# Graph layer with a feed-forward block: one one-hot for each gathered chunk, a VectorE lead of 20 products, a message ring of 16

## The chip, the cores and the metric

The kernel runs on one core of one Trainium2 chip. The metric is device time in microseconds (us), as the median of several executions. The profile shows one execution. Its engines are PE (TensorE, matmuls; PEld is its weight load), DVE (VectorE), ACT (ScalarE), POOL (GpSimd) and SP (SyncE).

## What is computed

12,500 nodes with 256 features each, and 212,500 edges (200,000 and one self loop for each node), sorted by destination. Cut to what matters:

```
xn  = layernorm(x)
agg = segment_sum(edge_weight[:, None] * xn[src], dst)     # the gather and scatter
gnn = relu(((1 + eps) * xn + agg) @ W1.T + b1) @ W2.T + b2
mix = hyperbolic mixer of xn (1x1 convolutions, batch norm over nodes, tanh/atanh maps)
x   = x + gnn + mix
x   = x + ffn(layernorm(x))   # top half of the nodes by a routing weight: gelu(. @ w1 + b1) @ w2 + b2
```

## The kernel before, in words

The nodes are worked through in 49 steps of 256 nodes (two tiles of 128 rows). The edges of a step lie in a window of 35 chunks of 128 edges. The 256 destinations of a step fall into four quarters of 64. For each chunk, POOL gathers 128 rows of `xn` from HBM into a buffer of the ring `msg` (an indirect DMA, L936). DVE makes a one-hot, 128 edges by 64 destinations, times the edge weights, in the ring `sel` (`edge` in `main_vector`, L1131). PE multiplies one-hot (as weights, 128x64) by messages (128x256) and sums into the quarter's 64 partitions of the bank `agg` (`edge` in `main_tensor`, L1328). One such pair of quarter and chunk is a **product**; the table `PRODUCTS` has 45 for a step. A quarter of an even number is side 0 (output partitions 0 to 63), one of an odd number side 1 (64 to 127). Chunks 7 to 9, 15 to 18 and 24 to 26 reach two quarters, so that 35 chunks make 45 products.

- The order of PE is written out by hand: `step` in `main_tensor` sends products up to certain counts (`PE_AT`) and puts the other work between: `mix_qkv` (L1351, L1352) at 0 and 12, `tail_supT` (L1380) at 0, `tail_w1` (L1388) at 2, `tail_w2` (L1397) at 6, `mix_h1` (L1342) at 16, 22 and 25, `mix_outT` (L1362) at 18 and 28, `mix_ft` (L1372) at 20 and 32, and the feed-forward block (L1423, L1435) at 28, 32, 35, 38, 41 and 45. I call what lies between two such counts a **burst**: products 0 and 1, 2 to 5, 6 to 11, and so on, the last one 41 to 44.
- 42 steps hold a feed-forward block (`FFN_AT`); steps 0, 1, 8, 17, 26, 35 and 44 don't, and their products 32 to 44 are one burst. Seven blocks stand behind the last step.
- The order of DVE is a loop over k = 0 to 44: at k it first makes the one-hot of product k + `LEAD` (12), then the work that `DVE_AT` puts at k: `take_sup` (L1188, the sums of the step before with the node's own row) at 0, `add_b2` (L1193) at 4, `mix_f` (L1178 to L1182) at 5, `ffn_result` (L1111) at 6, `mix_scale` (L453 to L455, L1138) at 6 and 12, `combine` (L1198 to L1203) at 7 and 15, `mix_recip`, `mix_ratio`, `mix_om` (L1143 to L1155) at 8 to 10 and 16 to 18, `mix_c` (L453, L1162, L1163) at 15 and 22, `mix_ft` (L1167) at 17 and 36, `tail_out` (L1214 to L1217) at 25 and 30, and the conversion of the next window's destinations (L1122) at 30.
- POOL gathers in the order in which the products first name the chunks (`GATHERS`); a chunk's number in it is its **place** (0 to 34). Gather number G may overwrite a buffer when the chunk that is `RING` (18) gathers back, and all before it, are done with (`FREED`, counted by the semaphore `slot_used`). The one-hot ring has `SEL_RING` (22) buffers of 64 columns.

The line that sets how far DVE may run ahead of PE, and the one that sets POOL's:

```
dve.wait_ge(slot_used, RING + max(0, at_ - SEL_RING + 1))
pool.wait_ge(slot_used, RING + back * STEP_PRODUCTS + FREED[m] + 1)
```

Of the kernel before, what the change touches and what calls it, by code (L numbers as in the profile page):

```python
# [7 lines left out]
ALU = mybir.AluOpType  # L8
ACT = mybir.ActivationFunctionType
F32 = mybir.dt.float32  # L10
# [4 lines left out]
P = 128  # L15
D = 256
# [3 lines left out]
HC = HID // P  # L20
RING = 18
SEL_RING = 22
LEAD = 12
EARLY_EDGES = 12
WINDOWS = 2
# [15 lines left out]
def products():  # L41


    order = []
    for h in range(2):
        for left, right in itertools.zip_longest(LEFT[h], RIGHT[h]):
            order += [(2 * h + side, k) for side, k in enumerate((left, right)) if k is not None]
    return order


PRODUCTS = products()
STEP_PRODUCTS = len(PRODUCTS)
GATHERS = list(dict.fromkeys(k for _, k in PRODUCTS))
PLACE = {k: n for n, k in enumerate(GATHERS)}
LAST_USE = {k: max(n for n, (_, kk) in enumerate(PRODUCTS) if kk == k) for k in GATHERS}
FIRST_OF = {q: min(n for n, (qq, _) in enumerate(PRODUCTS) if qq == q) for q in range(4)}
LAST_OF = {q: max(n for n, (qq, _) in enumerate(PRODUCTS) if qq == q) for q in range(4)}
FREED = [max(LAST_USE[k] for k in GATHERS[:n + 1]) for n in range(SLOTS)]


# [15 lines left out]
def build(nc, a, out):  # L76
# [3 lines left out]
    NS = NT // 2  # L80
# [8 lines left out]
    with ExitStack() as ctx:  # L89
        def sb(name, shape, dt=F32):  # L90
            return ctx.enter_context(nc.sbuf_tensor(name, shape, dt))
# [20 lines left out]
        window_dst = [sb(f"window_dst{b}", [P, SLOTS]) for b in range(WINDOWS)]  # L112
        rings = sb("rings", [P, RING * D + SEL_RING * P // 2])
        msg = [rings[:, D * q:D * (q + 1)] for q in range(RING)]
        H = P // 2
        sel = [rings[:, RING * D + H * q:RING * D + H * (q + 1)] for q in range(SEL_RING)]
        rem_msg = sb("rem_msg", [P, D])
# [674 lines left out]
        def x3_rows(m, h):  # L792
# [3 lines left out]
        DVE_AT = dict(scale=(6, 12), out=(8, 16), c=(15, 22), ft=(17, 36), sup=0, n4=1, f=5, y=6, x=4,  # L796
                      combine=(7, 15), rstd=20, tail_out=(25, 30), stage=30)

# [315 lines left out]
        def main_vector(dve):  # L1114
# [10 lines left out]
            def edge(i, n):  # L1125
                b, at_ = i % WINDOWS, i * STEP_PRODUCTS + n
                q, k = PRODUCTS[n]
                dve.wait_ge(slot_used, RING + max(0, at_ - SEL_RING + 1))
                if n == 0:
                    dve.wait_ge(dst_ready, i + 1)  # L1130
                v.tensor_scalar(sel[at_ % SEL_RING], iota[:, q * H:(q + 1) * H], window_dst[b][:, k:k + 1],  # L1131
                                window[b][:, k, 2:3].bitcast(F32), ALU.is_equal, ALU.mult).then_inc(sel_ready, 1)

# [86 lines left out]
            def step(i, j, mm):  # L1220
                mix = Link(dve, mix_link, MIX_LINKS, i)
                tail = Link(dve, tail_link, TAIL_LINKS, j)
                last = i == NS - 1
                for k in range(STEP_PRODUCTS):
                    if k == DVE_AT["stage"] and not last:
                        start_step(i + 1)
                    ahead = k + LEAD
                    nxt = ahead >= STEP_PRODUCTS
                    if not (last and nxt) and not (i == 0 and ahead < EARLY_EDGES):
                        edge(i + nxt, ahead % STEP_PRODUCTS)  # L1230
# [64 lines left out]
        def main_tensor(pe):  # L1295
# [20 lines left out]
            def edge(i, n):  # L1316
# [6 lines left out]
                if n == STEP_PRODUCTS - 1:  # L1323
                    remainder(i, 0)
                    remainder(i, 1)
                pe.wait_ge(sel_ready, i * STEP_PRODUCTS + n + 1)
                pe.wait_ge(msg_landed[gathered % RING], 16 * (gathered // RING + 1))
                te.matmul(agg[h][side * H:(side + 1) * H], sel[(i * STEP_PRODUCTS + n) % SEL_RING], msg[gathered % RING],  # L1328
                          start=first, stop=n == STEP_PRODUCTS - 1, skip_group_check=True).then_inc(slot_used, 1)
# [474 lines left out]
```

## Time and profile before

| | |
|---|---|
| median of 3 runs | 2653.31 us (2650.08 to 2653.38) |
| the profiled execution | 2652.74 us, its span 2651.0 us |
| PE busy | 2470.1 us (93%) |
| DVE busy | 1848.6 us (70%) |
| POOL busy | 1668.7 us (63%) |
| ACT busy | 1433.9 us (54%) |
| mean granted clock of PE | 0.982 |

The span runs from the first to the last instruction; 1.7 us of the execution lie around it. "Busy" is the union of an engine's instructions. A row of the waits tells how long an engine sat idle and what ended it; a row of the chain of waits is a piece of the path that ended last.

### The profile page before, as it was taken

What the parts mean: (1) busy time and instruction counts of PE and PEld (TensorE: products, weight loads), DVE (VectorE), ACT (ScalarE), POOL (GpSimd) and SP (SyncE); (2) the same over time, 40 slices, a digit from 0 to 9 for tenths busy, and PEclk for the clock granted to TensorE, in tenths of its full rate; (3) what the DMA queues carried; (4) which work ended last, traced back from release to release, by engine and by line L of the source; (5) the groups of instructions that cost most, each with busy time, mean ns of one, the idle gap of its engine ahead of it and who ended that gap; (6) DMA issues with size and microseconds to landing.
All of it is one profiled execution on the core that took longest, in us unless ns stands there. A gap on an engine that the chain in (4) does not pass through costs nothing.

```text
span 2651.0 us, 44955 instructions
## 1 busy us (share of the span) xinstructions
PE 2470.1 (93%) x13536; PEld 1775.5 (67%) x13536; DVE 1848.6 (70%) x6385; ACT 1433.9 (54%) x3219; POOL 1668.7 (63%) x1834
## 2 busy tenths in 40 slices
PE   4778999999999998999999999999899999999997
PEld 4665667666666665666666666666666666666686
DVE  7857676776766768667667676676776766767657
ACT  3545564655645646556455565564555655656531
POOL 1246777767677677676676766767767667677500
PEclk9889999999999999999999999999999999999998
DMA  6733434434344344443343433434434334343338
GB/s 204 249 105 104 127 111 121 112 111 128 107 113 117 103 123 115 114 118 107 111 120 108 131 110 109 119 105 116 121 112 118 111 107 120 109 131 110 93 115 276
DMA packets 225221, 327.46 MB, mean 124 GB/s; under 512 B 80846, under 2 KB 168511, under 8 KB 224957
## 3 DMA queue, kind: packets, MB, share of 16 engines
q0 software_dynamic: 84656, 231.94, 30.7%
q1 hardware_dynamic: 140300, 92.36, 11.6%
q8 instruction: 122, 2.00, 0.3%
q14 instruction: 143, 1.16, 0.1%
HBM read 285.70 MB, written 38.45 MB: 122 GB/s over the span
## 4 chain that ended last, share of the span: by engine, by line
PE 70%; DVE 20%; ACT 4%; DMA 3%; issue 2%; SPq 0%; DVEq 0%
PE bank L1328 16%; PE qkv L1423 13%; PE bank L1435 12%; PE bank L1342 8%; PE bank L1372 7%; DVE rings L1131 4%; PE qkv L1352 3%; DMA work<-in_x 3%; PE bank L1388 2%; PE bank L1397 2%; PE qkv L1351 2%; PE bank L1362 1%; DVE work L525 1%; DVE work L496 1%; DVE work L1198 1%
## 5 line engine op out<-in xcount | busy, mean ns | idle before, releaser
L936 POOL DMA_INDIRECT rings<-xn_dram,window x1715 | 1641.1, 957 | 753.6 <-issue 384.7
L1328 PE MATMUL bank<-rings 128*64 128x256 f32 x4410 | 700.8, 395 | 23.8 <-DVE rings L1131 21.9
L1131 DVE TENSOR_SCALAR rings<-iota,window_dst,window 128x64 f32<-128x64 f32 x2205 | 610.5, 332 | 32.5 <-PE bank L1328 17.8
L1328 PEld LDWEIGHTS bank<-rings 128*64 128x64 f32 x4410 | 302.9, 136 | 313.0 <-issue 121.3
L1435 PE MATMUL bank<-ffn_weights,work 128*128 128x256 f32 x1568 | 375.1, 388 | 0.0
L1423 PE MATMUL qkv<-work,ffn_weights 128*128 128x256 f32 x1568 | 367.3, 382 | 0.0
L1435 PEld LDWEIGHTS bank<-ffn_weights,work 128*128 128x128 f32 x1568 | 286.8, 190 | 82.0 <-issue 32.3
L1423 PEld LDWEIGHTS qkv<-work,ffn_weights 128*128 128x128 f32 x1568 | 290.4, 190 | 51.8 <-ACT work L1026 16.1
L1026 ACT ACTIVATE work<-qkv,fb 128x256 f32<-128x256 f32 x392 | 159.7, 472 | 303.2 <-PE qkv L1423 302.6
L1342 PE MATMUL bank<-resident,weights 128*128 128x256 f32 x1176 | 295.3, 394 | 0.0
L1342 PEld LDWEIGHTS bank<-resident,weights 128*128 128x128 f32 x1176 | 213.2, 191 | 79.2 <-issue 55.7
L1008 ACT ACTIVATE work<-bank 128x512 f32<-128x512 f32 x49 | 29.3, 597 | 433.6 <-PE bank L1380 394.7
L1351 PE MATMUL qkv<-ident,work 128*128 128x128 f32 x588 | 166.5, 283 | 62.5 <-ACT work L972 61.4
L1188 DVE SCALAR_TENSOR_TENSOR work<-work,cols,bank 128x512 f32<-128x512 f32 x49 | 36.6, 748 | 257.3 <-PE bank L1328 257.3
L1352 PE MATMUL qkv<-weights,work 128*128 128x128 f32 x1176 | 209.5, 282 | 0.0
L953 ACT ACTIVATE work<-qkv 128x1536 bf16<-128x1536 f32 x98 | 142.2, 1451 | 122.7 <-PE qkv L1352 122.7
L1372 PE MATMUL bank<-weights,work 128*128 128x256 f32 x784 | 195.7, 393 | 11.1 <-DVE work L1198 8.7
L1039 ACT ACTIVATE work<-bank,cols 128x256 f32<-128x256 f32 x294 | 149.8, 565 | 76.7 <-PE bank L1342 76.7
L1352 PEld LDWEIGHTS qkv<-weights,work 128*128 128x128 f32 x1176 | 186.8, 200 | 3.1
L1372 PEld LDWEIGHTS bank<-weights,work 128*128 128x128 f32 x784 | 141.6, 190 | 66.6 <-ACT work L983 34.9
L1351 PEld LDWEIGHTS qkv<-ident,work 128*128 128x128 f32 x588 | 86.5, 147 | 87.6 <-issue 85.0
L1193 DVE TENSOR_TENSOR work<-work,b_row 128x512 f32<-128x512 f32 x49 | 34.2, 698 | 135.0 <-DMA work<-in_x 134.9
(261 smaller groups left out, 3296.8 us busy)
## 6 DMA issues: line engine op xcount, KB each, us to landing
rings<-xn_dram,window POOLq DMA_INDIRECT x1715
xn_dram<-work SPq DMA_DIRECT2D x14, 896.0 KB, 8.7
work<-xn_dram SPq DMA_DIRECT2D x49, 256.0 KB
work<-in_x SPq DMA_DIRECT2D x48, 256.0 KB
out<-work SPq DMA_DIRECT2D x48, 256.0 KB
work<-in_x SPq DMA_DIRECT2D x7, 896.0 KB, 6.0
rings<-in_x SPq DMA_DIRECT2D x6, 896.0 KB, 10.9
rings<-out SPq DMA_DIRECT2D x6, 896.0 KB, 9.2
```

The costliest lines, as they stand in the source:

```text
L936: nc.gpsimd.indirect_dma_start(out=msg[G_ % RING][:, :], out_offset=None, in_=xn_dram[:, :], in_offset=bass.IndirectOffsetOnAxis(ap=window ...
L953: s.activation(sq_dump, qkv.rearrange("p r i s c -> p (r i s c)"), ACT.Square, accum_out=nsq[h]).then_inc(nsq_ready, 1)
L1026: ins = s.activation(hT[:, k], HID_BANK[q][:, e * D:(e + 1) * D], ACT.Gelu_apprx_tanh, bias=fb1[:, k:k + 1])
L1039: ins = s.activation(h2T[:, k], H1_BANK[q][:, e * D:(e + 1) * D], ACT.Relu, scale=bn_a[:, k:k + 1], bias=bn_b[:, k:k + 1])
L1131: v.tensor_scalar(sel[at_ % SEL_RING], iota[:, q * H:(q + 1) * H], window_dst[b][:, k:k + 1], window[b][:, k, 2:3].bitcast(F32), ALU.is_eq ...
L1328: te.matmul(agg[h][side * H:(side + 1) * H], sel[(i * STEP_PRODUCTS + n) % SEL_RING], msg[gathered % RING], start=first, stop=n == STEP_PR ...
L1342: ins = te.matmul(H1_BANK[q][:, e * D:(e + 1) * D], wqkvT[:, c, k * P:(k + 1) * P], h0T[:, c, 2 * i * P:2 * (i + 1) * P], start=(c == 0), ...
L1351: te.transpose(qkv[:, k // 2, k % 2, 0, :], lhs, ident[:, :])
L1352: ins = te.matmul(qkv[:, k // 2, k % 2, 1, :], lhs, mixW[:, k, :], start=True, stop=True)
L1372: ins = te.matmul(FT_BANK[h][:, 0:D], outT[:, c], wresT[:, c], start=(c == 0), stop=(c == 3))
L1423: ins = te.matmul(HID_BANK[q][:, e * D:(e + 1) * D], fw1[:, c, k * P:(k + 1) * P], x3T[:, c], start=(c == 0), stop=(c == C - 1))
L1435: ins = te.matmul(Y_BANK[:, h * D:(h + 1) * D], hT[:, k, h * P:(h + 1) * P], fw2[:, k], start=(k == 0 and h == 0), stop=(k == HC - 1), ski ...
```

## The change

- Each pair of products takes its side-1 product first (`products`). The order of the gathers changes with it.
- One one-hot for each chunk: where a chunk reaches two quarters, DVE makes it once, 128 columns wide, at the first of its two products, and nothing at the second. PE takes 64 of the columns for each product.
- The one-hot ring is 30 units of 64 columns, given out in a run by `one_hot_places`; a wide one takes two neighbouring units. A one-hot is held until its chunk's last product.
- `LEAD` is 20 in place of 12; one-hots for products 12 to 19 of step 0 are made ahead of the loop.
- The message ring has 16 buffers in place of 18 (the two rings together keep their size).
- The conversion of the next window's destinations moves from k = 30 to k = 22.

```
-RING = 18
-SEL_RING = 22
-LEAD = 12
+RING = 16
+SEL_UNITS = 30
+LEAD = 20
...
-            order += [(2 * h + side, k) for side, k in enumerate((left, right)) if k is not None]
+            order += [(2 * h + side, k) for side, k in ((1, right), (0, left)) if k is not None]
...
+FIRST_USE = {k: min(n for n, (_, kk) in enumerate(PRODUCTS) if kk == k) for k in GATHERS}
+REACHES = {k: sorted(q for q, kk in PRODUCTS if kk == k) for k in GATHERS}
...
+def one_hot_places(steps):
+    place, freed, holds, at = {}, {}, [-1] * SEL_UNITS, 0
+    for i in range(steps):
+        for k in GATHERS:
+            n = len(REACHES[k])
+            units = range(at % SEL_UNITS, at % SEL_UNITS + n)
+            assert units.stop <= SEL_UNITS
+            place[i, k], freed[i, k] = units.start, max(holds[u] for u in units) + 1
+            for u in units:
+                holds[u] = i * STEP_PRODUCTS + LAST_USE[k]
+            at += n
+    return place, freed
...
-                      combine=(7, 15), rstd=20, tail_out=(25, 30), stage=30)
+                      combine=(7, 15), rstd=20, tail_out=(25, 30), stage=22)
...
-                q, k = PRODUCTS[n]
-                dve.wait_ge(slot_used, RING + max(0, at_ - SEL_RING + 1))
+                if FIRST_USE[k] < n:
+                    return
+                quarters = REACHES[k]
+                dve.wait_ge(slot_used, RING + SEL_FREED[i, k])
...
-                pe.wait_ge(sel_ready, i * STEP_PRODUCTS + n + 1)
+                pe.wait_ge(sel_ready, gathered + 1)
```

The sequences that the table now gives for the end of a step, as (quarter, chunk), products 36 to 44:

```
before  (2,22) (3,34) (2,23) (3,24) (2,24) (3,25) (2,25) (3,26) (2,26)
change  (3,34) (2,22) (3,24) (2,23) (3,25) (2,24) (3,26) (2,25) (2,26)
```

PE, the last burst of a step with a feed-forward block (step 5), before; the number in `msg_landed` is the message buffer, so that 10 is chunk 25 and 11 is chunk 26:

```order
L1435 MATMUL bank<-ffn_weights,work 128x256 x3
L1328 MATMUL bank<-rings 64x256 [waits msg_landed10,sel_ready] x2
L1328 MATMUL bank<-rings 64x256 [waits msg_landed11,sel_ready]
L1311 TENSOR_LOAD work
```

The same place in the change; 14 is chunk 24, 0 is chunk 25 and 1 is chunk 26:

```order
L1463 MATMUL bank<-ffn_weights,work 128x256 x3
L1356 MATMUL bank<-rings 64x256 [waits msg_landed14,sel_ready]
L1356 MATMUL bank<-rings 64x256 [waits msg_landed1,sel_ready]
L1356 MATMUL bank<-rings 64x256 [waits msg_landed0,sel_ready]
L1339 TENSOR_LOAD work
```

Behind the register instructions that follow comes product 44, (2,26), in both. The burst was side 1, 0, 1, 0, with chunk 25 for both sides first; it is now side 0, 1, 0, 0.

DVE from the second `tail_out` (k = 30) to `take_sup` of the next step (k = 0), before:

```order
L1217 TENSOR_SCALAR route_w<-work,cols 128x1
L1131 TENSOR_SCALAR rings<-iota,window_dst,window 128x64 x6
L1167 SCALAR_TENSOR_TENSOR work<-bank,work,bres_row 128x256
L1131 TENSOR_SCALAR rings<-iota,window_dst,window 128x64 x9
L1188 SCALAR_TENSOR_TENSOR work<-work,cols,bank 128x512
```

The same stretch in the change (L1155 makes the one-hots, L1192 is `mix_ft`, L1213 `take_sup`):

```order
L1242 TENSOR_SCALAR route_w<-work,cols 128x1
L1155 TENSOR_SCALAR rings<-iota,window_dst,window 128x64 x4
L1155 TENSOR_SCALAR rings<-iota,window_dst,window 128x128
L1155 TENSOR_SCALAR rings<-iota,window_dst,window 128x64
L1192 SCALAR_TENSOR_TENSOR work<-bank,work,bres_row 128x256
L1155 TENSOR_SCALAR rings<-iota,window_dst,window 128x128
L1155 TENSOR_SCALAR rings<-iota,window_dst,window 128x64
L1155 TENSOR_SCALAR rings<-iota,window_dst,window 128x128 x4
L1213 SCALAR_TENSOR_TENSOR work<-work,cols,bank 128x512
```

Fifteen narrow one-hots (six ahead of `mix_ft`, nine behind it) have become twelve (six and six), of which six are wide.

DVE from `add_b2` (k = 4) to `ffn_result` (k = 6), before:

```order
L1193 TENSOR_TENSOR work<-work,b_row 128x512
L1131 TENSOR_SCALAR rings<-iota,window_dst,window 128x64
L1178 TENSOR_SCALAR work<-work 128x2
L1179 TENSOR_SCALAR work<-work 128x2
L1180 RECIPROCAL work<-work 128x2
L1181 TENSOR_TENSOR work<-work 128x2
L1182 SCALAR_TENSOR_TENSOR work<-work 128x2
L1131 TENSOR_SCALAR rings<-iota,window_dst,window 128x64
L1111 TENSOR_TENSOR resident<-bank,fb_row 128x2x256
```

In the change the first of the two one-hots is gone (product 25 is the second of chunk 16):

```order
L1218 TENSOR_TENSOR work<-work,b_row 128x512
L1203 TENSOR_SCALAR work<-work 128x2
L1204 TENSOR_SCALAR work<-work 128x2
L1205 RECIPROCAL work<-work 128x2
L1206 TENSOR_TENSOR work<-work 128x2
L1207 SCALAR_TENSOR_TENSOR work<-work 128x2
L1155 TENSOR_SCALAR rings<-iota,window_dst,window 128x64
L1133 TENSOR_TENSOR resident<-bank,fb_row 128x2x256
```

## Rows read from the trace of the kernel before

**Rows 1.** The page: busy times, and the chain that ended last, by engine

```profile
PE 2470.1 (93%) x13536; PEld 1775.5 (67%) x13536; DVE 1848.6 (70%) x6385; ACT 1433.9 (54%) x3219; POOL 1668.7 (63%) x1834
...
PE 70%; DVE 20%; ACT 4%; DMA 3%; issue 2%; SPq 0%; DVEq 0%
```

**Rows 2.** Busy us (and instructions) of each engine in one step with a feed-forward block

```profile
1322.63:1371.57 48.94, 47.70 (x263) 33.71 (x264) 33.79 (x114) 27.96 (x61) 33.72 (x35) 1.00 0.40 112
```

**Rows 3.** PE's waits: line, releaser, us in total, times, longest us

```profile
PE qkv L1351 <- ACT work L972: 61.4, 48, 7.3
...
PE bank L1328 <- DVE rings L1131: 21.9, 19, 1.8
...
PE bank L1372 <- DVE work L1198: 8.7, 32, 1.0
...
PE bank L1372 <- ACT work L983: 1.3, 7, 0.2
```

**Rows 4.** The chain that ended last, 1346 to 1379 us: start, us, what

```profile
1346.11 1.01 PE bank L1328 x4
...
1361.69 1.01 PE bank L1328 x6
...
1370.48 1.01 PE bank L1328 x8
1371.50 3.65 PE bank L1435 x16
...
1378.02 0.58 PE bank L1328 x4
```

**Rows 5.** Timeline, the same kind of step: ACT, DVE and PE around the seed

```profile
1331.64 0.20 ACT L959 ACTIVATE work<-work 128x1 f32<-128x1 f32 x1
...
1331.88 0.16 DVE L453 TENSOR_TENSOR work<-work 128x1 f32<-128x1 f32 x1
...
1344.15 1.97 PE L1372 MATMUL bank<-weights,work 128*128 128x256 f32 x8 [0.25 <-DVE work L1198]
```

**Rows 6.** DVE groups by form: whole span (first two), then 590.1 to 598.6 us

```profile
L1131 DVE TENSOR_SCALAR rings<-iota,window_dst,window 128x64 f32<-128x64 f32 x2205 | 610.5, 332 | 32.5 <-PE bank L1328 17.8 <-DVE work L1182 0.3 <-DVE work L1203 0.3
L1214 DVE TENSOR_SCALAR resident<-work 128x256 f32<-128x256 f32 x98 | 42.8, 437 | 0.0
...
L1131 DVE TENSOR_SCALAR rings<-iota,window_dst,window 128x64 f32<-128x64 f32 x23 | 5.6, 342 | 0.0
```

**Rows 7.** The chain that ended last, from step 8 to step 9

```profile
598.62 0.67 DVE work L1188
...
604.27 0.31 DVE rings L1131
...
610.84 0.30 PE qkv L1351
```

**Rows 8.** POOL's timeline: steps 8 and 9, and a stretch with DVE idle

```profile
587.12 0.94 POOL L936 DMA_INDIRECT rings<-xn_dram,window  x1 [1.26 <-PE bank L1328]
588.68 0.94 POOL L936 DMA_INDIRECT rings<-xn_dram,window  x1 [0.61 <-PE bank L1328]
...
601.23 0.95 POOL L936 DMA_INDIRECT rings<-xn_dram,window  x1 [0.30 <-issue]
...
1316.58 0.95 POOL L936 DMA_INDIRECT rings<-xn_dram,window  x1 [0.30 <-PE bank L1328]
...
1321.58 0.95 POOL L936 DMA_INDIRECT rings<-xn_dram,window  x1 [0.30 <-issue]
```

**Rows 9.** Timeline of POOL and PE, steps 0 to 2

```profile
214.44 0.94 POOL L936 DMA_INDIRECT rings<-xn_dram,window  x1 [1.27 <-PE bank L1328]
216.03 0.94 POOL L936 DMA_INDIRECT rings<-xn_dram,window  x1 [0.64 <-PE bank L1328]
...
276.86 0.62 PE L1328 MATMUL bank<-rings 128*64 128x256 f32 x2 [0.80 <-DMA rings<-xn_dram,window]
```

**Rows 10.** The chain that ended last: the gather that step 2 waits for

```profile
272.50 4.22 DMA rings<-xn_dram,window
```

More of the change, by code:

```diff
@@ L112, in build, with one_hot @@
         window_dst = [sb(f"window_dst{b}", [P, SLOTS]) for b in range(WINDOWS)]
-        rings = sb("rings", [P, RING * D + SEL_RING * P // 2])
+        rings = sb("rings", [P, RING * D + SEL_UNITS * P // 2])
         msg = [rings[:, D * q:D * (q + 1)] for q in range(RING)]
         H = P // 2
-        sel = [rings[:, RING * D + H * q:RING * D + H * (q + 1)] for q in range(SEL_RING)]
+        SEL_AT, SEL_FREED = one_hot_places(NS)
+        def one_hot(i, k, first, n):
+            at = RING * D + (SEL_AT[i, k] + first) * H
+            return rings[:, at:at + n * H]
         rem_msg = sb("rem_msg", [P, D])
@@ L1125, in edge @@
             def edge(i, n):
-                b, at_ = i % WINDOWS, i * STEP_PRODUCTS + n
-                q, k = PRODUCTS[n]
-                dve.wait_ge(slot_used, RING + max(0, at_ - SEL_RING + 1))
+                b, k = i % WINDOWS, PRODUCTS[n][1]
+                if FIRST_USE[k] < n:
+                    return
+                quarters = REACHES[k]
+                dve.wait_ge(slot_used, RING + SEL_FREED[i, k])
                 if n == 0:
                     dve.wait_ge(dst_ready, i + 1)
-                v.tensor_scalar(sel[at_ % SEL_RING], iota[:, q * H:(q + 1) * H], window_dst[b][:, k:k + 1],
-                                window[b][:, k, 2:3].bitcast(F32), ALU.is_equal, ALU.mult).then_inc(sel_ready, 1)
+                v.tensor_scalar(one_hot(i, k, 0, len(quarters)), iota[:, quarters[0] * H:(quarters[-1] + 1) * H],
+                                window_dst[b][:, k:k + 1], window[b][:, k, 2:3].bitcast(F32),
+                                ALU.is_equal, ALU.mult).then_inc(sel_ready, 1)
             def mix_scale(i, h, link):
@@ L1223, in step @@
                 last = i == NS - 1
+                if i == 0:
+                    for n in range(EARLY_EDGES, LEAD):
+                        edge(0, n)
                 for k in range(STEP_PRODUCTS):
@@ L1228, in step @@
                     nxt = ahead >= STEP_PRODUCTS
-                    if not (last and nxt) and not (i == 0 and ahead < EARLY_EDGES):
+                    if not (last and nxt):
                         edge(i + nxt, ahead % STEP_PRODUCTS)
@@ L1325, in edge @@
                     remainder(i, 1)
-                pe.wait_ge(sel_ready, i * STEP_PRODUCTS + n + 1)
+                pe.wait_ge(sel_ready, gathered + 1)
                 pe.wait_ge(msg_landed[gathered % RING], 16 * (gathered // RING + 1))
-                te.matmul(agg[h][side * H:(side + 1) * H], sel[(i * STEP_PRODUCTS + n) % SEL_RING], msg[gathered % RING],
+                te.matmul(agg[h][side * H:(side + 1) * H], one_hot(i, k, REACHES[k].index(q), 1), msg[gathered % RING],
                           start=first, stop=n == STEP_PRODUCTS - 1, skip_group_check=True).then_inc(slot_used, 1)
```

## The prediction

> **What bounds the kernel now.** I read the page first: PE is busy for 93% of the span, and the chain that ended last lies on it for 70%, on DVE for 20% [rows 1]. Then one step with a feed-forward block, an FFN step: it takes 48.94 us, 47.70 of them with PE busy, while DVE is busy for 33.79 [rows 2]. So in 42 of 49 steps PE bounds, and what is taken off DVE can give back only PE's waits. These are few [rows 3]: 61.4 us for ScalarE's L972 (48 times), 21.9 us for the one-hots of L1131 (19 times), 8.7 us for `combine` (L1198, 32 times). The 21.9 us are not spread evenly: 19 waits stand in the seven steps without a feed-forward block, three in each of steps 8, 17, 26, 35 and 44 (about 3.4 us a step), the rest at the start. So there are three sums to make: the FFN step, the step without, and the start. The reader should see in [rows 4] that PE's own price of a product depends on its neighbour.
>
> **The FFN step: the new order of sides.** Nothing is removed from PE; products and their two passes each stay. But a product fills half of the array's columns. Two products of different sides cost 0.58 us as a burst (0 and 1), four that alternate 1.01 us, while products 20 and 21, both side 1, cost 1.01 us for two [rows 4]. Three that alternate also cost 1.01 us (the x6 row). So a burst costs 0.15 us and 0.43 us for each product of its fuller side. I counted this for every burst of both orders. It changes in one: products 41 to 44 were side 1, 0, 1, 0 and cost 1.01 us; they are now 0, 1, 0, 0, three on side 0, which makes 0.15 + 3 x 0.43 = 1.44 us. Behind that burst stands L1435 without a gap [rows 4], so PE isn't waiting for anything there that could hide it, and `take_sup` and all that follows it start from the burst's end. **+0.43 us in 42 steps: +18.1 us.** In the seven other steps products 32 to 44 are one burst with seven products of side 0 before and after; there the order costs nothing, or 0.2 us at its end, where DVE is late anyway. Bounds: 0 if the array takes the last product alongside something else, 0.43 by the rows; I take 0.43, as the row of products 20 and 21 is the same case.
>
> **The FFN step: fewer one-hots.** Ten of the 45 instructions go, ten of the 35 left are wide. What is gained on the path is small. The 0.96 us wait at L1351 ends with ScalarE's L972, and the chain to it runs through ScalarE's seed L959, which ends at 1331.84, and DVE's L453, which starts at 1331.88 [rows 5]: DVE waits for ScalarE there, and is free only just in time. Between k = 4 and k = 6 one one-hot of two goes, but DVE can't start earlier than the seed: 0 us. The wait at L1372 (0.25 us in the row) ends with `combine` at k = 15. From `combine` at k = 7 to it there were eight one-hots, now seven. That frees about 0.3 us, but then L1372 waits for ScalarE's copy L983, as it does now in 7 steps for 1.3 / 7 = 0.19 us [rows 3]. So 31 steps gain (8.7 - 1.0) / 31 - 0.19 = 0.06 us: **-1.9 us.** The six waits of DVE for PE that become tighter (a one-hot made at k now waits for product k - 4 to k - 12, where it was k - 10) cost nothing: at k = 0 to 10 `take_sup` has already waited for the step's last product, from k = 18 on `mix_ft` has waited for product 19, and from k = 25 to 44 DVE is behind PE.
>
> **The step without a block.** Here DVE is the bound: from k = 23 to `take_sup` it works without a gap (590.15 to 598.62), and the chain runs from there through the load of x, DVE, ScalarE and L1351 at 610.84 [rows 7]. The lead of 20 lets PE finish its products without the 3.4 us of waits, but then PE waits for `take_sup` or L972. So what counts is DVE's own time. Of 23 one-hots in that stretch (5.6 us, 0.24 each) 18 are left: -1.2 us. Six of them are wide. The trace before has no 128-column one-hot; the same operation with 256 columns takes 437 ns against 332 for 64 [rows 6], 0.55 ns a column, so 64 more cost 0.035 us, and six 0.2 us (bounds: 0, and 0.105 each, the whole difference). Behind `take_sup` the one-hot at k = 5 goes, 0.31 us on the chain [rows 7]. Sum -1.3 us a step, in five steps: **-6.5 us** (bounds -4 and -8). In the Trainium skill, "VectorE: DVE Perf Modes", section on the TRN2 errata, the fixed part of a VectorE instruction is about 150 cycles of 0.96 GHz. By that a one-hot would cost an estimated 0.19 us and this term -5.3 us; the trace has 0.24, and I go by it.
>
> **The ring of 16.** A gather is a place later in the queue, and chunks are held over two products, so it is places 31 to 34 that suffer: they waited for products 16, 18, 22 and 24 and now for 23, 25, 27 and 29. In an FFN step POOL has room: 35 gathers at 1.255 us (below) are 43.9 of 48.94 us [rows 2], and the 5 us that are left take up a delay of 3.4 before the messages are due: nothing. From step 8 to 9, place 32 waits for product 25, which is of the same pair as product 26, for which the first gather of step 9 waited until 587.12. So place 32 runs at 587.12, and the second gather of step 9 four places later, 587.12 + 4 x 1.255 = 592.1 in place of 588.68 [rows 8]: 3.4 us later. The gather of place 11 goes from 601.23 to 604.7, lands by 608.9 at the 4.22 us of [rows 10], and its burst ends by 609.5; L1351 is due at 610.84 - 1.3 = 609.5. Covered, but without room: if `take_sup` came still earlier, this would be the bound.
>
> At the start nothing covers it. From 216.03 to 272.50 POOL issues back to back, 45 intervals of 1.255 us, and step 2 waits for the last of these at 276.86 [rows 9, 10]. The same arithmetic holds: place 32 of step 0 at 214.44, the second gather of step 1 at 219.5 in place of 216.03: **+3.4 us** at step 2, where PE is then bound by itself. Whatever DVE gives in steps 0 and 1 lies beside this.
>
> By the Trainium skill, "GPSIMD Engine Reference", section 1 (Specifications), GpSimd's SBUF interfaces are shared with VectorE and contend with some of its modes. By that fewer one-hots should quicken POOL, and the start would lose less. The trace doesn't show it: with DVE busy ten gathers from 588.68 to 601.23 take 1.255 us each, with DVE idle four from 1316.58 to 1321.58 take 1.25 [rows 8]. I take nothing.
>
> **The rest.** In the last step PE waits for DVE at L1362 and L1372; one one-hot less: -0.2 us. The conversion at k = 22 runs where DVE waits for ScalarE: 0. The one-hots for products 12 to 19 ahead of step 0 are made while PE and ScalarE work through `mix_qkv`: 0; uncovered they would be 5 one-hots, 1.2 us.
>
> Sum: 18.1 - 1.9 - 6.5 + 3.4 - 0.2 = +12.9 us. The profiled execution took 2652.7 us, 0.6 us below the median of the runs, so the median becomes 2653.3 + 12.9 = 2666 us. A difference under 0.2% (5.3 us) I call none.
>
> **The rivals.**
> 1. *The order of sides costs nothing* (0.13). PE might take the last product of the burst alongside the one before, or the 0.43 us might be taken from the 0.96 us wait that follows. Against it: products 20 and 21, and the chain from burst to `take_sup` and to that wait. The sum without it is -5.2 us, 2648. This decides the sign: the change is faster as soon as the term is under 5.2 us, or 0.12 us a step.
> 2. *The gathers bound steps 9, 18, 27, 36 and 45* (0.10). Place 11 lands with no room to spare; were it 1.3 us later, the gain of 6.5 us is gone: 2672.5. For it: 4.22 us of landing is one gather's; others share their time with the loads of x. Against it: most land quicker.
> 3. *The seed comes earlier after all* (0.05). If the DVE relief reached the 0.96 us wait in 41 steps it could give up to 39 us: 2627. Against it: [rows 5].
> 4. *The change doesn't lift the lead* (0.04): the ring of 30 units holds a wide one-hot so long that DVE stands at k - 4 and PE keeps its waits for L1131. The step without a block gains nothing, 2672.5.
>
> **How the numbers follow.** My forecast (0.68) with its bounds, the start from 2.5 to 4.5, the five steps from -4 to -8, FFN steps from -2 to 0, covers 2661 to 2671. The range 2656 to 2674 takes in rivals 2 and 4 and part of what lies between the forecast and rival 1. Slower: forecast, rivals 2 and 4, 0.80 after a little for their lower edge. Rival 1 lies at the edge of no change and is halved, so no change 0.10 with that edge, faster 0.10 with rival 3.
>
> **What would show it.** The last burst of an FFN step reads 1.44 in place of 1.01 us on the chain; an FFN step is 49.3 us long; PE's waits for one-hots are gone, and a wait for the gathered rows has come in steps 1, 2 and 9; L1351's 0.96 us stays; DVE is busy about 100 us less. Step 9's L1351 comes some 12 us after `take_sup`, as now. If the FFN step stays at 48.9 us, I am wrong in the main term; if it is shorter, rival 3 was right.

## The result, and the profile after

| | median, us | runs | profiled execution, us (span) | mean granted clock |
|---|---|---|---|---|
| before | 2651.77 (2650.08 to 2653.38) | 5 | 2652.74 (2651.0) | 0.982 |
| changed | 2662.94 (2660.97 to 2666.09) | 5 | 2661.82 (2659.7) | 0.984 |

The ratio is 1.0042, with a 95% interval of 1.0027 to 1.0057: slower by 11.2 us, where 12.9 were forecast. (With two more runs of the kernel before, its median came down from the 2653.31 on which the forecast was built.) Line numbers shift: the one-hots are L1155, the products L1356, `take_sup` L1213, the transposes of `mix_qkv` L1379, `combine` L1223, the transposes of the output L1390, `mix_ft` L1400, the gathers L958.

The page of the changed kernel, busy times and chain, against [rows 1]:

```profile
PE 2487.2 (94%) x13536; PEld 1783.6 (67%) x13536; DVE 1749.9 (66%) x5895; ACT 1433.9 (54%) x3219; POOL 1671.3 (63%) x1834
...
PE 73%; ACT 13%; DVE 9%; DMA 2%; issue 2%; SPq 0%; POOL 0%; DVEq 0%
```

VectorE works 98.7 us less with 490 instructions fewer; TensorE, with the same 13536 matmuls, works 17.1 us more (the products alone 16.9: 700.8 us before, 717.7 now). The relief went to an engine that did not bound, the loss to the one that did. The groups by line and form say where each comes from:

```profile
L1356 PE MATMUL bank<-rings 128*64 128x256 f32 x4410 | 717.7, 394 | 17.8 <-DVE rings L1155 7.2 <-issue 6.0 <-DMA rings<-xn_dram,window 4.7
L1155 DVE TENSOR_SCALAR rings<-iota,window_dst,window 128x64 f32<-128x64 f32 x1225 | 356.1, 336 | 9.2 <-PE bank L1356 0.3
L1155 DVE TENSOR_SCALAR rings<-iota,window_dst,window 128x128 f32<-128x128 f32 x490 | 170.2, 361 | 307.5 <-PE bank L1356 305.7
```

A wide one-hot takes 361 ns against 336 for a narrow one, so the second 64 columns cost 25 ns, where the prediction interpolated 35.

One step with a feed-forward block, from `take_sup` to `take_sup` (the columns of [rows 2]), and the chain around its last burst, against [rows 4] (in a row of the chain x8 counts matmul instructions, two for each product):

```profile
1326.90:1376.15 49.25, 48.16 (x263) 33.97 (x264) 31.45 (x104) 27.95 (x61) 33.66 (x36) 1.00 0.39 111
```

```profile
1350.30 1.01 PE bank L1356 x4
...
1361.21 1.01 PE bank L1356 x8
...
1374.67 1.44 PE bank L1356 x8
1376.11 3.65 PE bank L1463 x16
```

The last burst (1374.67) takes 1.44 us for four products, where a burst of four alternating ones (1361.21) takes 1.01.

PE's waits, against [rows 3]:

```profile
PE qkv L1379 <- ACT work L994: 55.4, 48, 7.3
...
PE bank L1356 <- DVE rings L1155: 7.2, 10, 1.4
PE bank L1408 <- DVE work L1213: 6.5, 5, 1.6
PE bank L1356 <- issue: 6.0, 5, 1.4
...
PE bank L1390 <- DVE work L1180: 5.0, 2, 3.9
PE bank L1356 <- DMA rings<-xn_dram,window: 4.7, 8, 1.1
PE bank L1400 <- DVE work L1223: 1.2, 2, 1.0
```

The waits for one-hots fell from 21.9 to 7.2 us and those for `combine` from 8.7 to 1.2. Behind each of the five steps without a block PE now waits for `take_sup` (L1408) instead. Of the 4.7 us for gathered rows 4.2 lie in step 1 and 0.5 in step 9; in step 2, where the prediction had one too, there is none.

To compare many kernels I use one ledger, worked out from each trace: the starts of the 49 `take_sup` cut the main part into 48 intervals. "Step 1" is the first of them. The five steps without a block (8, 17, 26, 35, 44) stand with the step behind each, as five pairs. Then come 35 more steps with a block (3 to 47 without the pairs), and the last interval, step 48; step 2 is counted with the rest. Differences of the changed kernel against the one before:

| | before, us | changed, us | difference | forecast, in the same cut |
|---|---|---|---|---|
| step 1 | 40.64 | 44.29 | +3.65 | +3.4 |
| five pairs | 447.52 | 439.45 | -8.07 | 5 x (-1.3 + 0.39) = -4.6 |
| 35 FFN steps | 1712.66 | 1724.08 | +11.42 | 35 x 0.39 = +13.5 |
| last interval | 48.28 | 50.00 | +1.72 | -0.2 + 0.39 = +0.2 |
| the rest | 401.87 | 401.84 | -0.03 | +0.4 |
| span | 2650.97 | 2659.67 | +8.70 | +12.9 |

(0.39 is the forecast's 18.1 - 1.9 over 42 steps. The +3.4 of the start was forecast for step 2; it stands here in step 1, where it shows.)

### The profile page after: what moved, and what is told of

Read it like the earlier page. It is cut to its first block, busy times and chain, and to the rows that moved or that the text cites. A ratio compares the mean times of both kernels' runs of the same rounds, so it can differ in the third digit from the quotient of the medians.

```text
span 2659.7 us, 44369 instructions
## 1 busy us (share of the span) xinstructions
PE 2487.2 (94%) x13536; PEld 1783.6 (67%) x13536; DVE 1749.9 (66%) x5895; ACT 1433.9 (54%) x3219; POOL 1671.3 (63%) x1834
## 4 chain that ended last, share of the span: by engine, by line
PE 73%; ACT 13%; DVE 9%; DMA 2%; issue 2%; SPq 0%; POOL 0%; DVEq 0%
PE bank L1356 17%; PE bank L1463 14%; PE qkv L1451 13%; PE bank L1370 11%; PE bank L1400 7%; PE qkv L1380 5%; PE qkv L1379 3%; PE bank L1390 2%; ACT work L975 2%; ACT work L988 1%; DVE rings L1155 1%; DMA work<-in_x 1%; ACT work L991 1%; ACT work L1005 1%; ACT work L989 1%
## 5 line engine op out<-in xcount | busy, mean ns | idle before, releaser
L958 POOL DMA_INDIRECT rings<-xn_dram,window x1715 | 1643.5, 958 | 765.6 <-issue 372.9
L1356 PE MATMUL bank<-rings 128*64 128x256 f32 x4410 | 717.7, 394 | 17.8 <-DVE rings L1155 7.2
L1155 DVE TENSOR_SCALAR rings<-iota,window_dst,window 128x64 f32<-128x64 f32 (+1 forms) x1715 | 496.3, 343 | 316.7 <-PE bank L1356 306.0
L1356 PEld LDWEIGHTS bank<-rings 128*64 128x64 f32 x4410 | 312.6, 136 | 314.3 <-issue 137.0
L1370 PEld LDWEIGHTS bank<-resident,weights 128*128 128x128 f32 x1176 | 213.0, 191 | 78.9 <-issue 55.4
L1379 PE MATMUL qkv<-ident,work 128*128 128x128 f32 x588 | 165.4, 281 | 56.5 <-ACT work L994 55.4
L1400 PE MATMUL bank<-weights,work 128*128 128x256 f32 x784 | 195.2, 392 | 6.3 <-DVE work L1223 1.2
L1400 PEld LDWEIGHTS bank<-weights,work 128*128 128x128 f32 x784 | 140.9, 189 | 62.4 <-ACT work L1005 31.1
L1379 PEld LDWEIGHTS qkv<-ident,work 128*128 128x128 f32 x588 | 86.0, 146 | 81.6 <-issue 79.0
L475 DVE TENSOR_TENSOR work<-work 128x1 f32<-128x1 f32 (+2 forms) x309 | 50.5, 163 | 103.4 <-ACT work L1000 73.3
```

Source lines behind the costliest of these rows:

```text
L958: nc.gpsimd.indirect_dma_start(out=msg[G_ % RING][:, :], out_offset=None, in_=xn_dram[:, :], in_offset=bass.IndirectOffsetOnAxis(ap=window ...
L1155: v.tensor_scalar(one_hot(i, k, 0, len(quarters)), iota[:, quarters[0] * H:(quarters[-1] + 1) * H], window_dst[b][:, k:k + 1], window[b][: ...
L1356: te.matmul(agg[h][side * H:(side + 1) * H], one_hot(i, k, REACHES[k].index(q), 1), msg[gathered % RING], start=first, stop=n == STEP_PROD ...
L1370: ins = te.matmul(H1_BANK[q][:, e * D:(e + 1) * D], wqkvT[:, c, k * P:(k + 1) * P], h0T[:, c, 2 * i * P:2 * (i + 1) * P], start=(c == 0), ...
L1379: te.transpose(qkv[:, k // 2, k % 2, 0, :], lhs, ident[:, :])
L1400: ins = te.matmul(FT_BANK[h][:, 0:D], outT[:, c], wresT[:, c], start=(c == 0), stop=(c == 3))
```

## The experiments

Theory: the loss is the order of sides in one burst, by the rule of 0.15 us and 0.43 us for each product of the fuller side; the one-hots give a little in five steps. Rival: the order costs nothing, and the loss lies in the ring, the lead or the wide one-hots. What the ledger gave in all of them ("own" is the mean of the five steps without a block alone):

| kernel | `take_sup` of step 1 | own | five pairs | FFN step, median | last | span |
|---|---|---|---|---|---|---|
| before | 263.84 | 41.72 | 447.5 | 48.92 | 48.28 | 2651.0 |
| changed | 267.03 | 40.65 | 439.5 | 49.25 | 50.00 | 2659.7 |
| order alone | 265.10 | 41.91 | 446.5 | 49.35 | 50.34 | 2668.5 |
| before, one burst clustered | 264.54 | 41.77 | 447.8 | 49.36 | 48.66 | 2666.7 |
| changed, burst alternates | 266.03 | 40.77 | 439.5 | 48.85 | 49.91 | 2643.8 |
| changed, two narrow for a wide | 267.83 | 41.83 | 442.1 | 49.25 | 50.48 | 2664.2 |
| changed, lead 12 | 269.35 | 41.20 | 441.9 | 49.25 | 50.08 | 2664.1 |
| changed, lead 12, ring 18 | 265.30 | 41.10 | 448.5 | 49.25 | 50.05 | 2666.4 |
| before, ring 16 | 265.50 | 41.81 | 441.0 | 48.92 | 49.94 | 2648.2 |
| paired products | 264.38 | 40.26 | 437.1 | 48.48 | 49.65 | 2626.1 |
| paired, lead 12, ring 18 | 264.33 | 40.58 | 441.5 | 48.42 | 49.44 | 2628.4 |
| even bursts | 263.11 | 40.43 | 434.8 | 48.01 | 49.69 | 2606.6 |
| before with even bursts | 258.94 | 41.33 | 440.7 | 48.01 | 47.99 | 2605.1 |
| even, later turn | 261.86 | 40.64 | 431.7 | 47.77 | 49.03 | 2591.4 |

### The order of sides, three ways

The order of the change alone, in the kernel before:

```
-            order += [(2 * h + side, k) for side, k in enumerate((left, right)) if k is not None]
+            order += [(2 * h + side, k) for side, k in ((1, right), (0, left)) if k is not None]
```

> The kernel before with the order of products of the change (side 1 of a pair first) and with nothing else of it: narrow one-hots, one for each product, lead 12, ring of 18. My theory: the whole loss of the feed-forward steps comes with it, 42 x 0.33 to 0.43 us = 14 to 18 us: 2666 to 2670, more than the full change, since the 5 steps without a feed-forward block gain nothing. Rival (the order costs nothing, the loss is in the wide one-hots, the lead or the ring): 2652.

Measured, within the theory's 2666 to 2670: 2668.59 us (2665.9 to 2673.1), ratio 1.0065 (1.0052 to 1.0077) to the kernel before at 2651.26. The FFN step is 49.35 us, 0.43 more, and its last burst on the chain reads:

```profile
1377.55 1.44 PE bank L1328 x8
1378.99 3.65 PE bank L1435 x16
```

The kernel before with nothing but two neighbours of its table exchanged, so that its last burst is 0, 0, 1, 0:

```
+    order[40], order[41] = order[41], order[40]
     return order
```

> The kernel before with products 40 and 41 exchanged, so that its burst of products 41 to 44 has three products of one side and one of the other; nothing else of the change is in it. My theory: +0.43 us in each of 42 feed-forward steps, 2651.8 becomes about 2670 (at 0.33 us a step, 2666). Rival (the order costs nothing by itself): 2652.

Measured: 2668.65 us (2662.91 to 2672.03), ratio 1.0062 (1.005 to 1.0074). FFN step 49.36 us, burst 1.44:

```profile
1377.26 1.44 PE bank L1329 x8
```

The same exchange in the changed kernel. Products 40 and 41 are (3, 25) and (2, 24) there and change places, so that the last burst goes from side 0, 1, 0, 0 to 1, 1, 0, 0: two products of each side, but not in the two alternating pairs of which the expectation speaks:

> The changed kernel with products 40 and 41 of the order exchanged, so that the burst of products 41 to 44 of each step has the sides 1, 0, 0 and 0 replaced by two alternating pairs again; all else stays. My theory (a burst costs 0.15 us and 0.43 us for each product of its fuller side): each step with a feed-forward block is 0.43 us shorter, 49.25 us becomes 48.82, and 42 of them give 18 us: 2662.9 becomes about 2645, 7 us under the kernel before. By the traces alone, which show 49.25 against 48.92, at least 0.33 x 42 = 14: 2649. Rival (the sides' order costs nothing, and the loss comes from the wider one-hots, the lead or the ring): the time stays at 2663. In the profile the chain's first 64-column burst behind the take of the sums would go from 1.44 to 1.01 us.

Measured: 2645.61 us (2641.36 to 2646.91), ratio 0.9976 (0.9965 to 0.9986). FFN step 48.85 us, 0.40 less than the changed kernel's, and the burst:

```profile
1366.27 1.02 PE bank L1357 x8
```

The two products of one side stand next to each other here, and the burst still costs what an alternating one does. So what counts is how many products of a burst fall on its fuller side, and not which product stands beside which. The kernel with paired products (below) has the same four sides in its last burst, and reads the same:

```profile
1359.17 1.02 PE bank L1359 x8
```

One line of a table of numbers turns the sign of the whole change: with it the change is 17.3 us faster than without, and 5.7 us faster than the kernel before. The rival is excluded in both directions.

### What the one-hots and the lead give

The changed kernel, each wide one-hot written by two narrow instructions at the same place:

```
+                for m, q in enumerate(quarters):
+                    ins = v.tensor_scalar(one_hot(i, k, m, 1), iota[:, q * H:(q + 1) * H], ...
```

> The changed kernel, but each one-hot of 128 columns is written by two instructions of 64 columns, one behind the other, at the same place of the order; lead, ring and order of products as changed. My theory: only fewer instructions on VectorE gain anything. The five steps without a feed-forward block lose their gain (40.65 us back to about 41.75), and each feed-forward step the 0.07 us by which the changed kernel (49.25) lies under the kernel with the order alone (49.32): 5 x 1.1 + 42 x 0.07 = 8 us, 2663 becomes about 2671; VectorE's busy time goes from 1750 to about 1850 us. Rival (the gain came from the longer lead, not from fewer instructions): 2663.

Measured: 2665.54 us (2659.7 to 2666.47), ratio 1.0049 (1.0036 to 1.0062). VectorE is busy 1841.7 us in 6385 instructions, and the steps without a block are back at 41.83 us: in them it is the number of instructions that counts, not the lead, as expected. But the FFN steps stay at 49.25, so their 0.10 us against the order alone (49.35) does not hang on the wide form. The total rises by 2.6 us, with overlapping intervals, and not by 8. In this trace no step behind one without a block has its clock lowered after PE's wait at `mix_qkv` (below), where the changed kernel's has two, which gives back some 3 us of it.

The changed kernel with `LEAD = 12`:

> The changed kernel with a lead of 12 products in place of 20. My theory: the lead itself is worth little, since behind the products PE waits for the take of the sums in any case; PE's waits for one-hots come back in the five steps without a feed-forward block (7 us in all become some 15), and two more one-hots stand in VectorE's unbroken stretch there, 0.5 us a step: 2663 becomes about 2665. Rival (the lead carries the gain of the five steps, about 1.1 us each, or the late start): 2668 and more, or, if the lead makes the start late, about 2661.

Measured: 2665.01 us (2660.17 to 2665.86), ratio 1.0047 (1.0033 to 1.006). PE's waits for one-hots rise from 7.2 to 12.9 us, and the steps without a block from 40.65 to 41.20, the two one-hots of 0.24 us that now stand in VectorE's unbroken stretch. Here too the FFN steps stay at 49.25.

```profile
PE bank L1356 <- DVE rings L1155: 12.9, 12, 1.3
PE bank L1356 <- DMA rings<-xn_dram,window: 8.6, 10, 1.8
```

What the 0.10 us comes from shows in the wait for `combine`: 9.0 us (29 times) with the order alone, 1.9 (4 times) with two narrow ones, 1.2 (twice) in the changed kernel. Between its two `combine` VectorE makes eight one-hots with the order alone, and seven in both others, all of them narrow: at a lead of 20 the second use of a chunk, for which nothing is made any more, falls into this stretch. One one-hot less there is enough. At the lead of 12 there are five, two of them wide, and they bring no more (49.25 us). The earlier conversion of the destinations was not tried alone.

### The rings

The kernel before with `RING = 16` and `SEL_RING = 30`:

> The kernel before with a message ring of 16 places in place of 18 (the room goes to the ring of one-hots, 30 in place of 22, lead 12 as before). My theory: the smaller ring costs only at the start, where the sums of step 1 come 2.8 to 3.4 us later (263.84 us becomes about 267), and nothing behind it: about 2655. Rival A (the late start comes from the order and the one-hots, not from the ring): 2652. Rival B (the ring also binds after each of the 5 steps without a feed-forward block, about 1.2 us each): about 2661.

Measured: 2650.1 us (2648.68 to 2654.91, 11 runs) against 2651.26 (19 runs), ratio 0.9999 (0.999 to 1.0008): no difference, where the theory had 2655. The sums of step 1 come 1.7 us later, less than the expected 2.8 to 3.4 and half as late as in the changed kernel (3.2), and the five pairs are 6.5 us shorter in this trace. So the ring's term was neither alone at the start nor visible in the end.

The changed kernel with lead 12 and a ring of 18:

```
-RING = 16
-SEL_UNITS = 30
-LEAD = 20
+RING = 18
+SEL_UNITS = 22
+LEAD = 12
...
-            assert units.stop <= SEL_UNITS
+            if units.stop > SEL_UNITS:
+                at += SEL_UNITS - at % SEL_UNITS
+                units = range(n)
```

> The changed kernel with a message ring of 18 places, a lead of 12 and 22 units for one-hots (a wide one that would lie over the end of the ring starts at its beginning). To be held against the kernel with a lead of 12 alone, which has the ring of 16. My theory, after the ring of 16 in the kernel before put the sums of step 1 1.7 us later and moved the time by less than can be measured: the sums of step 1 come 1.5 to 3 us earlier than with the ring of 16, and the time is 0 to 3 us less. Rival (the smaller ring binds more in the new order, since chunks are held over more places): 5 us or more less, with shorter steps 9, 18, 27, 36, 45.

Measured: 2666.69 us (2659.08 to 2668.97), ratio 1.0052 (1.0038 to 1.0066), against 2665.01 for the lead of 12 with a ring of 16. The sums of step 1 come 4.05 us earlier, more than the expected 1.5 to 3. Yet the total is the same: the pairs take 448.5 us in place of 441.9. That is where the gain went, and the windows show how. Stretches of 2.5 us behind step 8 (us, then PE, PEld, DVE, ACT, POOL busy, granted clock, DMA share, GB/s), first with the ring of 18:

```profile
607.90:610.40 2.50, 1.34 (x12) 0.59 (x10) 1.80 (x5) 2.44 (x4) 1.89 (x3) 1.00 0.39 107
610.40:612.90 2.50, 0.75 (x7) 0.78 (x8) 2.29 (x4) 1.60 (x4) 1.89 (x3) 1.00 0.37 110
612.90:615.40 2.50, 2.50 (x17) 2.09 (x17) 2.39 (x6) 0.42 (x1) 1.89 (x3) 0.63 0.35 100
615.40:617.90 2.50, 2.50 (x13) 1.45 (x10) 1.42 (x7) 2.40 (x7) 1.89 (x3) 0.69 0.35 105
```

and with the ring of 16 at the same lead:

```profile
612.30:614.80 2.50, 1.83 (x12) 0.71 (x10) 1.82 (x6) 2.36 (x4) 1.89 (x3) 1.00 0.30 85
614.80:617.30 2.50, 0.82 (x7) 0.58 (x6) 2.09 (x4) 1.80 (x4) 1.89 (x3) 1.00 0.36 103
617.30:619.80 2.50, 2.50 (x23) 1.92 (x21) 2.42 (x5) 0.83 (x1) 1.89 (x3) 1.00 0.37 107
619.80:622.30 2.50, 2.50 (x14) 1.64 (x12) 2.06 (x8) 2.32 (x8) 1.89 (x3) 1.00 0.35 105
```

PE idles for a few us ahead of `mix_qkv` in both; with the ring of 18 it idles some 0.5 us more, and the granted clock then falls to 0.5, its level of 1.2 GHz, over work that PE bounds. The steps 9, 18, 27, 36 and 45 take 48.07 to 49.54 us there; with the ring of 16 four of them take 46.67 to 47.18 and one, whose clock falls too, 48.47.

### A faster order, and the rule carried on

The changed kernel, with the exchange above and the burst of products 20 and 21 (both side 1 in [rows 4] and in the change) paired:

```
+    order[40], order[41] = order[41], order[40]
+    order[20:25] = [(1, 17), (2, 15), (1, 18), (2, 16), (3, 27)]
+    order[25:28] = [(3, 28), (2, 17), (3, 29)]
```

> The changed kernel with products 40 and 41 exchanged and products 20 to 27 put in the order 1, 2, 1, 2, 3, 3, 2, 3 of their quarters, so that the burst of products 20 and 21 has one product on each side and the later bursts stay paired. My theory (0.43 us for each product of a burst's fuller side): another 0.4 us less a feed-forward step than with products 40 and 41 alone (48.85 becomes about 48.43) and as much in the other steps where PE bounds, 2645.6 becomes 2625 to 2628, faster than the kernel before and the changed one. Rival (the pair 20 and 21 hides behind a wait of PE, or a gather or a one-hot becomes late): 2640 to 2646.

Measured: 2627.92 us (2626.02 to 2628.2), ratio 0.991 (0.9897 to 0.9923). FFN step 48.48 us: another 0.37 less.

The same with lead 12, 22 units and the ring of 18:

> The kernel with paired products, with a ring of 18, 22 units for one-hots and a lead of 12. The ring of 18 in the changed kernel put the sums of step 1 4 us earlier than the ring of 16 at the same lead, but the time did not fall: in each of the steps 9, 18, 27, 36 and 45 the granted clock of TensorE fell to 0.5 behind the wait at the transposes of mix_qkv, and these steps took 48.1 to 49.5 us. If it is the way in which PE idles there that decides where the clock falls (theory), the same happens here: all five of these steps near 48 us, and 2626 to 2631 in all. If those falls were chance (rival), two or three of the five show them and the earlier start is kept: about 2624.

Measured: 2630.52 us (2628.51 to 2632.6), ratio 0.9916 (0.9903 to 0.993), so nothing is gained. The granted clock falls behind PE's wait in all five of the steps in question (46.95 to 48.72 us), in the ring-16 version in three. With the run above that makes ten of ten in the two kernels with 18 message buffers, 22 units and lead 12, against two of five in the changed kernel and one of five in it with lead 12. In the run above the falls take back what the larger ring gave at the start. Here it gave nothing there (`take_sup` of step 1 at 264.33 us against 264.38), and the pairs are 4.4 us longer, the 35 steps 2.1 us shorter. Which of the three sizes brings this about was not tried apart; the kernel before, with its ring of 18, has two of five.

Bursts of three cost as much as bursts of four [rows 4], so I made the products 20 to 44 alternate strictly and cut them at even places:

```
+    right = [(q, k) for q, k in order[20:] if q % 2]
+    left = [(q, k) for q, k in order[20:] if q % 2 == 0]
+    order[20:] = [p for pair in itertools.zip_longest(right, left) for p in pair if p is not None]
...
-        PE_AT = dict(w1=2, w2=6, qkv=12, h1=(16, 22, 25), outT=(18, 28), ft=(20, 32), hid=35, y=(38, 41))
+        PE_AT = dict(w1=2, w2=6, qkv=12, h1=(16, 22, 26), outT=(18, 28), ft=(20, 32), hid=36, y=(38, 42))
```

> The changed kernel with products 20 to 44 strictly alternating between side 1 and side 0, and the bursts cut at even places: 22 to 25 and 26 and 27 in place of 22 to 24 and 25 to 27, 32 to 35, 36 and 37, 38 to 41 and 42 to 44 in place of 32 to 34, 35 to 37, 38 to 40 and 41 to 44. No product is added or removed. My theory (a burst costs 0.15 us and 0.43 us for each product of its fuller side) counts 23 such products in a step, where the kernel with paired products has 25, the kernel with only 40 and 41 exchanged 26 and the changed one 27: a feed-forward step of 48.48 us goes to about 47.65, and 2627.9 us becomes about 2590 (2585 to 2600). Rival (the rule holds for neighbours inside a burst only by chance of these bursts, or PE now waits for VectorE or ScalarE in each step and the gain stops there): 2610 or more, and PE's waits at the transposes of mix_qkv longer than 0.96 us a step.

Measured: 2608.33 us (2606.21 to 2611.71), ratio 0.9833 (0.982 to 0.9847). Outside the expected 2585 to 2600, and just under the rival's 2610: the FFN step is 48.01 us, not 47.65. Its waits say why; the first of these rows was two waits of 5.0 us in all in the changed kernel, the second two of 1.2:

```profile
PE bank L1393 <- DVE work L1183: 17.2, 50, 4.3
...
PE bank L1403 <- DVE work L1226: 12.8, 39, 0.9
```

PE has become quick enough to reach the output's transposes (L1393) ahead of VectorE in every step. The mean of 0.35 us misleads, as 5.7 of the 17.2 us lie in the last interval: in most FFN steps this wait is 0.19 us and the one for `combine` 0.32, which together cover the 0.36 that a step lacks.

The same order in the kernel before, with narrow one-hots, lead 12 and ring 18:

> The kernel before (one narrow one-hot for each product, lead 12, ring of 18) with the same even order and cuts as the kernel with even bursts. My theory: what the change brings beside its order is the difference between before with its own order and the changed kernel with 40 and 41 exchanged, 5.6 us; so this kernel lies about 6 us above the one with even bursts, at about 2596, by 1.1 us in each of five steps. Rival (once PE is quicker, VectorE's load comes onto the path of the feed-forward steps as well, and fewer one-hots are worth more): 10 us or more above it.

Measured: 2610.6 us (2606.88 to 2615.2), ratio 0.9846 (0.9833 to 0.986); 2.3 us above, with overlapping intervals. The FFN step is 48.01 us in both. So the fewer one-hots are worth nothing in those steps as they lie here: between its two `combine`, where PE waits, VectorE makes eight in both kernels. They give 0.9 us in each of the five steps without a block (41.33 against 40.43), and of these 4.5 us half shows in the medians. Both theories overstated it. The total is not clean, though: the two kernels also differ in ring and lead, and in the traces this one has the sums of step 1 4.2 us earlier.

At last the transposes that wait are put two products later:

```
-        PE_AT = dict(w1=2, w2=6, qkv=12, h1=(16, 22, 26), outT=(18, 28), ft=(20, 32), hid=36, y=(38, 42))
+        PE_AT = dict(w1=2, w2=6, qkv=12, h1=(16, 22, 26), outT=(18, 30), ft=(20, 32), hid=36, y=(38, 42))
```

> The kernel with even bursts, with the transposes of the second half's output (outT of h = 1) behind product 29 in place of product 27, so that the products 28 and 29 run before it. In the kernel with even bursts a feed-forward step takes 48.00 us, not the 47.65 that the count of products gives, and PE waits at these transposes in each step for VectorE, 17.2 us in 50 waits, 0.35 us each. Theory: that wait is what held back the rest of the gain, and two products (0.43 us) put ahead of it fill it: about 47.6 us a step and 2608.3 - 42 x 0.35 = about 2593. Rival (VectorE's own loop sets the step: it starts as much later as PE starts the transposes, and the next step moves with it): 48.0 us a step and 2608.

Measured: 2595.48 us (2593.22 to 2595.61), ratio 0.9788 (0.9775 to 0.9802), the fastest here, 2.1% under the kernel before. The FFN step is 47.77 us, 0.24 less than with even bursts and 0.17 above the expected 47.6, which had taken the wait as 0.35 us in each step where it mostly was 0.19. The wait is gone but in the last interval, where it was long before:

```profile
PE bank L1403 <- DVE work L1226: 13.0, 38, 0.9
PE bank L1393 <- DVE work L1183: 5.3, 2, 3.9
```

What is left at `mix_ft` for `combine` (L1403, 0.34 us in 38 steps) is the next thing to move.

## Why the prediction was right

- **The order of sides, +0.43 us in 42 steps.** Right in mechanism and size. Put into the kernel before, it costs 0.43 us an FFN step; taken out of the changed one, it gives 0.40. The order alone costs 17.3 us in all, for a forecast 18.1. The reading of [rows 4], that a burst costs 0.15 us and 0.43 for each product of its fuller side, carried over to bursts that no trace had shown. Only the words that a product's price "depends on its neighbour" go too far: side 1, 1, 0, 0 costs 1.02 us, as 1, 0, 1, 0 does. Rival 1, which had the greatest chance of the four, falls.
- **The FFN step's one-hots, -0.06 us in 31 steps.** The place was right (the wait for `combine`), the size under-counted: 0.07 to 0.10 us an FFN step, some 3 to 4 us in all where 1.9 were forecast. I let ScalarE's copy take over as the releaser, as in 7 steps before; it does so twice, 0.3 us in all. The 0.96 us wait for ScalarE stayed, as [rows 5] said: 55.4 us in 48 waits. Rival 3 falls.
- **The steps without a block, -1.3 us each.** Own time: 41.72 to 40.65, so -1.07 for a forecast -1.0. The price of a one-hot there comes out near the trace's 0.24 us: two more at a lead of 12 cost 0.55 us, 0.27 each, and six more when each of the six wide ones is made as two narrow, 1.18 us, 0.22 each when the 25 ns of each width are added back. (By the Trainium skill, "VectorE: DVE Perf Modes", the section on the TRN2 errata, the estimate was 0.19; the runs are above it.) From `take_sup` to `mix_qkv` it is 11.56 us (602.25 to 613.81) in place of 12.22 (598.62 to 610.84), -0.66 where -0.31 was forecast; the load of x on that chain, 3.79 us before and 3.47 now, accounts for the rest:

```profile
602.25 0.66 DVE work L1213
...
603.35 3.47 DMA work<-in_x
...
613.81 0.30 PE qkv L1379
```

 Two pairs that are undisturbed in both traces (steps 8 and 26) moved by -1.3 us, for a forecast -0.9. Rival 2 (gathers bound step 9) and rival 4 fall.
- **The ring, +3.4 us at the start.** The sum is right: `take_sup` of step 1 comes 3.2 us later and that of step 2 3.3. So is the way of the gathers: place 32 of step 0 runs at 214.23 us, for a forecast 214.44, the second gather of step 1 at 219.35, for 219.5, and the gather that step 2 waited for at 275.86 in place of 272.50. But PE waits in step 1 already and no longer for that gather, and the cause is not the ring alone. "Whatever DVE gives in steps 0 and 1 lies beside this" was wrong too. In the kernel before, the ring alone makes `take_sup` of step 1 1.7 us later and the order of sides alone 1.3, for which the prediction has no term of its own there; in the changed kernel with lead 12 the ring makes 4.05, and the lead of 20 takes 2.3 of them back. The terms do not add, and that they met 3.4 was partly luck. What nobody would see in the times: in the kernel before the smaller ring costs nothing in the end.
- **The last step, -0.2 us.** Wrong: +1.72. The sum had VectorE's chain get shorter, and it had no term for TensorE's clock. Before, the clock falls ahead of PE's last long wait, and in the changed kernel behind it, over work that nothing hides:

```profile
2495.00:2500.00 5.00, 4.47 (x21) 2.54 (x19) 4.75 (x13) 3.03 (x9) 3.78 (x4) 0.76 0.41 115
2500.00:2505.00 5.00, 3.33 (x18) 3.00 (x19) 3.65 (x15) 2.56 (x6) 0.95 (x1) 1.00 0.19 56
```

```profile
2503.00:2508.00 5.00, 1.29 (x11) 0.64 (x7) 4.86 (x10) 1.49 (x6) 3.78 (x5) 0.98 0.39 103
2508.00:2513.00 5.00, 4.76 (x18) 4.14 (x19) 3.02 (x16) 3.52 (x8) 2.12 (x3) 0.68 0.33 98
```

 The first fence is of the kernel before, the second of the changed one. That the same +1.7 stands in the order alone and in the ring of 16 alone (50.34 and 49.94 us) fits this: neither shortens nor lengthens VectorE's work there. So do all fourteen traces: in the three in which the fall lies ahead of this wait (the kernel before, the one with one burst clustered, the one with even bursts in the kernel before) the last interval takes 47.99 to 48.66 us, in the eleven others 49.03 to 50.48.
- **What the sum left out** is that term everywhere. Three of the five pairs differ by -3.1, -2.6 and +0.2 us where -0.9 was forecast, each with the clock lowered in one of the traces or both. The five pairs together favour the changed kernel by 3.5 us more than the forecast in these two executions. With the 2.1 us of the 35 steps and 0.2 of the start and the rest, and against the 1.5 of the last interval, that makes the +8.7 of the traces out of +12.9; the medians, at +11.2, lie nearer the sum. That the errors partly cancel is luck.

## What to carry to other kernels

Where an engine bounds the kernel, read its own instructions for prices that depend on what they are grouped with, and count them in every order that a table can give, before any buffer or lead is tuned: here an exchange of two entries was worth 17 us, and with three more changes of order and place 67 (2662.9 to 2595.5), while 99 us of VectorE's work were worth 2 to 6. A reordering that comes with a change for another reason has to be costed as a change of its own. When a gain at one place doesn't reach the total, look at the granted clock behind the bounding engine's waits before looking for a new wait.

## What was not expected of the hardware

The granted clock of TensorE falls to 0.5 (1.2 GHz) for 3.4 us, in a few places 6.8, in some of the steps in which PE has just idled, and what it costs depends on which side of PE's wait it falls. Behind step 35 of the changed kernel, with the clock falling behind the wait:

```profile
1905.90:1908.40 2.50, 1.84 (x12) 0.75 (x10) 1.80 (x5) 2.44 (x4) 1.89 (x3) 1.00 0.46 116
1908.40:1910.90 2.50, 0.88 (x6) 0.77 (x6) 2.20 (x4) 1.62 (x4) 1.89 (x3) 0.92 0.33 98
1910.90:1913.40 2.50, 2.50 (x14) 2.50 (x13) 2.43 (x5) 0.00 (x0) 1.89 (x3) 0.50 0.36 110
```

and behind step 8, with almost the same busy time of PE ahead of it, without:

```profile
609.80:612.30 2.50, 1.84 (x12) 0.65 (x8) 1.72 (x6) 2.44 (x5) 1.89 (x2) 1.00 0.37 107
612.30:614.80 2.50, 0.99 (x9) 1.02 (x10) 2.39 (x4) 1.36 (x3) 1.89 (x2) 1.00 0.39 105
614.80:617.30 2.50, 2.50 (x21) 1.82 (x21) 2.43 (x5) 1.27 (x1) 1.89 (x2) 1.00 0.38 105
```

The steps behind are 48.19 and 46.47 us long: 1.7 us for one fall. Where it comes ahead of the wait, as in four of the five pairs of the kernel with the later turn, the step behind is 44.9 to 46.2 us long, while in the fifth, with the clock falling behind the wait, it is 46.6. With six such places in the program, this can spread a kernel's executions by several us; only one execution of each was profiled, so that share of their spread is an estimate. What decides between the two was not settled.
